# Moving the key, mask and value loads of the next batch ahead of its query store in the DMA queue program

## What is computed

```python
Q = layernorm(x) @ WQ + bQ;  K = ctx @ WK + bK;  V = ctx @ WV + bV      # plain reshape to (b, 16, -1, 16)
attn = softmax((Q K^T) * mask) / 4
x = x + (attn V) @ Wp + bp
probs = softmax(layernorm_affine(x) @ Wr + br)                         # 8 experts; 1 to 7 share perturbed weights
x = x + p0 * ffn(h; W1, W2) + (1 - p0) * ffn(h; W1', W2')              # h = layernorm(x), gelu, 256 -> 1024 -> 256
```

## Time and profile before

| | us |
|---|---|
| median of three runs | 804.89 |
| lowest, highest | 800.08, 814.68 |
| the profiled execution's own time | 803.5 |
| its span in the profile | 801.7 |
| PE busy in it | 683.7 |
| mean granted PE clock, as a share of full speed | 0.882 |

### The profile page before, as it was taken

The page is one execution under the profiler, slowest core; times in us unless marked ns, Lnnn a source line. Parts: engine busy times, 40 slices in busy tenths (PEclk is TensorE's granted clock), DMA queues, the critical chain, the costliest instruction groups (busy, mean ns, idle before and its releaser), DMA issues.

```text
span 801.7 us, 13910 instructions
## 1 busy us (share of the span) xinstructions
PE 683.7 (85%) x5442; PEld 566.5 (71%) x5442; DVE 514.0 (64%) x988; ACT 369.3 (46%) x544; POOL 228.3 (28%) x210
## 2 busy tenths in 40 slices
PE   5457777998995799898898898899987999999995
PEld 4346576886784687687687677668765888888884
DVE  5879768759669865965865874866497343343441
ACT  2214235546554554555454644545533544455442
POOL 2224034354244244334325424514280000000000
PEclk9758658989998898998797898869898999999998
DMA  9951342333153051342324206130102112222211
GB/s 279 164 134 25 54 129 54 54 102 106 19 138 105 2 111 45 107 81 75 107 38 117 80 9 147 61 124 29 68 12 80 27 53 79 80 79 79 79 32 48
DMA packets 133041, 64.40 MB, mean 80 GB/s; under 512 B 105712, under 2 KB 123120, under 8 KB 132976
## 3 DMA queue, kind: packets, MB, share of 16 engines
q1 hardware_dynamic: 132976, 63.51, 30.4%
HBM read 36.21 MB, written 23.09 MB: 74 GB/s over the span
## 4 chain that ended last, share of the span: by engine, by line
PE 60%; DVE 20%; issue 6%; ACT 4%; DMA 4%; SPq 3%; POOL 1%; DVEq 0%; ACTq 0%; POOLq 0%
PE ps_y L340 6%; PE ps_y L341 6%; PE ps_y L342 6%; PE ps_h L340 5%; PE ps_h L342 5%; PE ps_h L341 5%; DVE region_a L1171 3%; PE ps_t L340 3%; DVE ind L1269 3%; PE ps_m L688 3%; PE ps_t L341 3%; PE ps_t L342 3%; PE ps_t L582 3%; PE ps_t L637 2%; ACT region_a L871 2%
## 5 line engine op out<-in xcount | busy, mean ns | idle before, releaser
L1080 POOL TENSOR_TENSOR region_c_lo<-region_b,region_c_hi 128x512 fp32r<-128x512 f32 x64 | 95.7, 1504 | 117.2 <-ACT region_c_hi L910 117.2
L907 ACT ACTIVATE region_b<-ps_h,bias 128x512 f32<-128x512 f32 x92 | 63.2, 687 | 117.9 <-PE ps_h L342 116.9
L1532 DVE TENSOR_TENSOR region_c_lo<-region_b,region_c_hi 128x512 fp32r<-128x512 f32 x64 | 44.1, 692 | 107.8 <-ACT region_c_hi L910 107.8
L1269 DVE TENSOR_SCALAR ind<-key,cand 128x2048 bf16<-128x2048 uint16 x124 | 100.1, 849 | 18.2 <-PE ps_m L688 17.3
L340 PE MATMUL ps_y<-region_c_hi,w_hi 128*128 128x512 f32 x256 | 106.3, 415 | 1.9 <-POOL region_c_lo L1080 1.6
L341 PE MATMUL ps_y<-region_c_lo,w_hi 128*128 128x512 f32 x256 | 103.5, 404 | 0.0
L342 PE MATMUL ps_y<-region_c_hi,w_lo 128*128 128x512 f32 x256 | 103.0, 402 | 0.0
L1062 POOL TENSOR_TENSOR region_a<-region_a,mx 128x1024 f32<-128x1024 f32 x32 | 67.3, 2104 | 87.2 <-DVE mx L1175 87.2
L340 PE MATMUL ps_h<-x2s_hi,w_hi 128*128 128x512 f32 x184 | 81.9, 445 | 5.3 <-DVE x2s_lo L1132 4.8
L688 PEld LDWEIGHTS ps_m<-ones_bf,ind 128*128 128x128 bf16 x1984 | 56.9, 98 | 34.2 <-DVE ind L1269 24.3
L688 PE MATMUL ps_m<-ones_bf,ind 128*128 128x1 bf16 x1984 | 62.5, 164 | 20.0 <-DVE ind L1269 18.5
(11 more groups left out here) (181 smaller groups left out, 1393.2 us busy)
## 6 DMA issues: line engine op xcount, KB each, us to landing
qs<-q_scr SPq DMA_DIRECT2D x16, 512.0 KB, 4.7
acc_scr<-acc SPq DMA_DIRECT2D x8, 514.0 KB, 5.1
acc<-acc_scr SPq DMA_DIRECT2D x8, 514.0 KB, 3.5
xa<-in_x SPq DMA_DIRECT2D x8, 512.0 KB, 6.0
q_scr<-qn_hi SPq DMA_DIRECT2D x16, 256.0 KB, 4.7
q_scr<-qn_lo SPq DMA_DIRECT2D x16, 256.0 KB, 5.3
x<-in_x SPq DMA_DIRECT2D x32, 128.0 KB, 4.3
xt_scr<-region_b SPq DMA_DIRECT2D x8, 512.0 KB, 2.9
```

The costliest lines, as they stand in the source:

```text
L907: act.activation(g[:, f % 4, :], hidden_in(e, b, f), ACT.Gelu_apprx_tanh, bias=bias[:, e, f:f + 1]).then_inc(s["gelu"].handle, 1)
L1080: pool.tensor_tensor(gs[1][:, f % 4, :], g[:, f % 4, :], gs[0][:, f % 4, :].bitcast(F32), ALU.subtract).then_inc(s["g_lo"].handle, 1)
L1269: dve.tensor_scalar(ind[s % 2][:], key[:, key_of[rnd][s], :], cand[:, s:s + 1], None, ALU.is_le).then_inc(ind_ready.handle, 1)
```

## The change

In SP's body the whole of `load_context(i + 1)` is moved from behind `load_queries(i + 1)` to ahead of `store_queries(i + 1)`. Nothing is added or taken away; the waits inside each of the three functions stay as they are.

```diff
@@ -481,9 +481,9 @@
                 load_x(i + 2)
             load_residual(i)
             if not last:
+                load_context(i + 1)
                 store_queries(i + 1)
                 load_queries(i + 1)
-                load_context(i + 1)
             else:
```

## The result

The changed kernel takes 770.14 us (median of four runs, 766.22 to 771.88), the kernel before 802.77 in the same comparison. The ratio is 0.961 with a 95% interval of 0.955 to 0.966; measured once more beside others, it is 0.959 (0.954 to 0.964). My forecast was 779 against 804.89, a ratio of 0.968: right in sign and mechanism, some 5 to 7 us too small. As an absolute time, 770.14 lies a little under the lower end of my range (771, and 772 for the forecast's own); the measured ratio applied to the 804.89 I had forecast against gives 773.

The account below looks back on a forecast made before the run. PE, busy 683.7 of 801.7 us, was taken to bound, held by late transfers and then a slow clock. 11.0 + 14.6 + 1.6 - 1.0 = 26.2 us off 803.5, plus 1.4 to the median: 779 us, range 771 to 795.

Parts of the forecast that it names:

- The move costs nothing on SP: SP's fourteen context issues, 8.9 us, fit into 21.2 us free ahead of the query store, so store and reload keep their time.
- Rival 4: SP issues the context too slowly ahead of the query store, making it late at seven handoffs: about 830 us; chance 0.03.
- Stalls of PE, 11.0 us: PE's idling ahead of the scores at seven handoffs, 11.3 us, goes except 0.3 us at handoff 5.
- Rival 2: The query reload replaces the key loads as PE's late transfer, some 3 us of stalls stay: 785 to 797 us; chance 0.10.
- DVE's wait for the mask is worth nothing by itself: DVE's 5.96 us idling at handoff 3 is no loss of that size: its next mask product again waits for PE.
- The clock, 14.6 us at handoffs 3 to 6: PE keeps full clock from first to second score tile, 6.9 us instead of 10.1 to 11.7: gain 14.6 us.
- Rival 1: The router's narrow products, not idling, lower PE's clock, so only stalls go: 794 us, partial form about 787; chance 0.20.
- The clock at handoff 1, 1.6 us: Half a clock fall saved on PE at handoff 1, where a count stands ahead of the scores: 1.6 us.
- Small waits behind PE, 1.0 us off: Small waits surfacing behind PE in round 1, a quarter of a microsecond at each of four handoffs: 1.0 us deducted.
- Rival 3: The gain at the second score tile is lost at the next body's start: about 801 us; chance 0.09.

Follow-up runs that it names:

- the context between store and reload: Whole context load placed between the query store and the query reload, against the kernel before the change: 856.5 us, ratio 1.071.
- The keys alone: Only the eight key transfers ahead of the query store, mask and values behind the reload, against the kernel before: ratio 0.960; one later traced execution 777.5 us.
- the mask alone: Only the four mask transfers ahead of the query store, keys and values behind the reload, against the kernel before: ratio 1.002.
- the filled stall: Kernel before with SP's order kept and 38 unused wide products on PE ahead of its wait for queries and keys at handoffs 1 to 6: ratio 0.980.
- handoff 0 alone: Context load ahead of the query store in body 0 only, other bodies as in the kernel before: one execution, 796.5 us.

## Why the prediction was right, and where its size was off

**The move costs nothing on SP.** Right. The store's issue follows its split as before, and 10 us lie between the last value transfer and the store. One reading of mine was off, without effect on the sum: keys and mask, issued by 335.6 with the store at 349.22, would have been 13.6 us ahead when issued and some 10 when landed, not in place 15 us ahead. Rival 4 did not appear; the context between store and reload shows what it would have cost.

**Stalls of PE, 11.0 us.** Right: 11.3 before and 0.38 after, so 10.9. The keys alone bring it, the mask alone does not. Only the place of the 0.3 us that stay was off: not for the reload at handoff 5, but for ACT at handoff 0. Rival 2 did not appear (no stall released by qs in the changed kernel; in the trace of the keys alone there is one, 0.36 us at handoff 6).

**DVE's wait for the mask is worth nothing by itself.** Right, by the mask alone: ratio 1.002.

**The clock, 14.6 us at handoffs 3 to 6.** Right: 6.92 to 6.93 us against the 6.9 that I had put together from handoff 2, and 10.14 to 11.70 before, 14.5 us in all. Rival 1 (the clock falls anyway) is refuted for these by the filled stall and by the traces of the changed order. In the five traces with the keys ahead of the store and PE's order unchanged there are 30 handoffs from 1 to 6, and two of them have a clock fall (8.58 us at one, behind the 0.36 us stall; 9.59 instead of 8.11 at another, with no stall). In the traces of the kernel before, of the mask alone and of handoff 0 alone there are 18 such handoffs, and 13 have a fall. That a short stall makes a fall likely, not certain, agrees with what the Trainium skill says in TensorE: Matmul & The Clock Gate, section "What's actually happening": activity releases the slow clock, and it is judged on a grid that runs free of the kernel.

A stall is not the only way to lose the clock, though: in body 7 of the changed kernel PE runs without a gap through a count and the router (at 521.93), and the granted clock is 0.50 from 524.8 to 531.

**The clock at handoff 1, 1.6 us.** This term was mis-sized: I took half a fall because a count stands ahead of the scores. It went from 11.30 to 8.11 us, 3.2 in all. Handoff 2, where the clock was up before too, gave another 0.3 (8.43 to 8.11). With a count ahead of the scores and no stall, the clock stayed up in four of those five traces. Body 7, where the clock fell without a stall, misled me. One difference is that no score tile stands there between the count and the router; no run tests whether that is what matters.

**Small waits behind PE, 1.0 us off.** Not seen. The stretches behind the second tile did not grow: in the two traces of the changed kernel the one behind handoff 3 takes 50.4 and 50.3 us, and before it took 52.6 with 2.1 of stall.

**What is left.** 10.9 of stalls and 18.1 between the tiles are 29.0 of the 37.3 us between the two spans (801.7 and 764.4). Another 8.3 us lie outside the handoffs, where I had forecast nothing. Part is the clock at the bodies' beginnings. The beginning of body 5 in the kernel before, and the same stretch (11.4 us behind the second tile) in the changed kernel:

```profile
388.00:391.00 3.00, 2.44 (x22) 1.68 (x19) 2.97 (x5) 0.45 (x2) 1.96 (x2) 0.50 1.00 289
```

```profile
368.70:371.70 3.00, 2.44 (x42) 1.63 (x34) 2.97 (x5) 1.03 (x3) 1.99 (x2) 1.00 0.98 255
```

The execution that was profiled was also the quickest of its four. By place, 2.0 of the 8.3 us lie ahead of handoff 0, 5.1 in the six stretches from a second tile to the next body's scores, and 1.2 behind the last second tile. In the second measurement of the changed kernel (span 769.7 us) the same reckoning gives 10.9 and 17.9, and 3.2 us outside; there the three places have 0.7, -0.3 and 2.8. In the trace of the keys alone (775.7) nothing lies outside (-0.9), and the whole difference to the kernel before is 26.0 us. So the gain outside the handoffs is not at the same place each time. That it is the clock's scatter fits the place ahead of handoff 0: the mean granted clock from 15 us to the second tile there is 0.66 in the kernel before, 0.73 in the changed kernel's first trace and 0.65 in that of the keys alone. Whether a part belongs to the change is open: the two ratios of 0.959 and 0.961 ask for 31 to 33 us, and the handoffs account for 29. Rival 3 (given back later) did not appear.

## What to carry to other kernels

Read a wait for a transfer on the engine that bounds, not on the one that waits longest: here 36 us of DVE's waits were worth nothing and 11 us of PE's were worth about three times their length, because the slow clock went with them. In a hand-written DMA order, put ahead of a store that waits for late data every load whose own conditions are long fulfilled; between that store and its reload was the worst place of those tried. A stall of one or two microseconds in front of thin matrix work should be priced with the slow clock behind it. If the stall cannot be moved, filling it with unused wide products may pay: here 38 of them won 16 us.

## What the runs showed of the hardware that was not expected

The time to issue the same transfers is not fixed: the fourteen context transfers took 8.9 to 10.3 us at the seven handoffs of the kernel before, behind the reload, and 10.5 to 11.2 directly behind the query store. Why is not shown. The same 1.2 us stall cost the slow clock in one execution (10.14 us between the tiles) and not in another (6.98). And one execution of the kernel with the keys first took 2082 us, with PE busy 2029 us over the usual number of products while the other engines' busy times were as always; nothing like it came in its other executions, and its cause is unknown. Its wide products started 0.84 us apart, where those of the other traces start 0.23 or 0.43 apart.
